# Layer 1 of a two-layer decoder: attention stages and helper threads reordered across batches, weights folded

## The chip, the cores and the metric

One core of a Trainium2 chip runs the whole decoder in one program. The metric is the device time in microseconds of that core; the median of three executions counts. All tensors are fp32 except one-hot tables, masks and an identity, which are bf16.

## The reference, cut to what matters

There are eight batches (B) of 256 tokens (T) with 256 features (D), and 16 heads of 16 features. Layer 0 (an attention, a convolved cross attention, a latent attention with a mixture of four experts) is not touched by the change. Between the layers stands a scan over the tokens of six-component line coordinates, which gives one gate per batch and token (`Gt`). Layer 1 computes, for each batch, with LN a layer norm without weights and post-norm residuals:

```
# attention ("tally" in the kernel), x = output of layer 0
q, k, v = split(x @ qkv_w.T + qkv_b)
y  = softmax(causal(q k.T / 4)) v + gate * (x @ memv_w.T + memv_b)
x2 = LN(x + y @ out_w.T + out_b)
# cross attention over 64 listed context tokens per query ("count")
cd = ctx @ W_kv_down.T ;  k, v = split(cd @ W_kv_up.T) ;  q = x2 @ W_q.T
# a key listed n times weighs n times; keys that are not listed are left out
z  = LN(x2 + (softmax over listed(q k.T / 4) v) @ W_out.T)
# feed-forward, 8 experts of width 64, two branches
Q = z @ W_Q.T ; K = cumsum(z) @ W_K.T            # the sum runs over tokens
fwd(Q, K):  sum_e w_e * ((Q V_e) * (K W_e)) U_e + w b,   w = softmax(gelu(Q r1) r2)
inv(Q @ W_inv, K @ W_inv):  the same form with its own weights
out = LN(z + ((fwd + alpha * inv) / n) @ W_O.T)   # n = number of the token
```

All products that precede an elementwise factor are linear in z or in its running sum, and all that follow are linear in the products. `W_Q V`, `W_Q W_inv V`, `W_K W`, `W_Q r1`, `U W_O` and `memv_w out_w` are therefore constant matrices.

## The kernel before, in words

Each engine (TensorE = PE, VectorE = DVE, ScalarE = ACT, GpSimd = POOL, SyncE = SP) has its own program, written out by Python generators. A stage of work is a generator per engine, and each `yield` ends a step. `weave` and `braid` take a step of a main generator and then the steps of the others that are due in proportion, the same way on each engine, so the order on every engine is fixed at build time. Semaphores link the engines.

**Attention** (`attention_pe`, `attention_dve`, `attention_act`, from L527 on) runs in slots of two heads. A slot i holds on TensorE: the scores of pair i (L573) with the mask added by an identity product (L583); the turning of the probabilities of an earlier pair into the flip bank (`flip_probs`, L620); and their product with the values into OA (`values`, L635). VectorE takes the row maxima (L752) and, in count attention, multiplies by the counts (L759). ScalarE takes the exponentials (L702, L704) and moves the flipped probabilities to SBUF (`move_probs`, L689). There are two score banks, SM[0] and SM[1], so the scores of pair i wait for the exponentials of pair i-1 (`bank_free`). Tally attention flips one slot behind the scores and has 8 + 1 + 1 = 10 slots; count attention flips two slots behind and has 11. With two flip banks ScalarE alternates exponential and move; with one bank (`early`, L709) it makes both moves and then both exponentials, and TensorE puts `values` between the two flips. Layer 1 uses two flip banks, PT[0] and PT[1]; layer 0 uses one.

**Layer 1.** `reader_*` is one chain per batch: turn X, q and k, v, the memory projection (L2428, L2430), tally attention with the hot sums between scores and flips (128 one-hot products into SC, L2451, from tables that VectorE compares, L2556, two groups of eight per slot), turn of Z and its addition (L2576), out projection, layernorm into X2, the q, k, v of the cross attention (through QF and a masking on ScalarE, L728), count attention, projection, layernorm into Zb. It has 35 steps, 21 of them attention slots. `feed_*` is the feed-forward of one batch with 22 steps: turn Zb (L359), fQ (FQ[0]), running sum and fK (FQ[1]), finv on both (FQ[2], FQ[3]), r1 on FQ[0] and FQ[2] with a gelu (L2720), eight factor products (L376, moved by L2727 and multiplied at L2759), router (L2655) and softmax, spreading the weights (L2673), the back product (L2681, L2683), scale, turn of Yb, fO added to Zb (L2702, L395), layernorm, store. It fills the banks PJ[0] and PJ[1] in turn. `stagger` runs reader 0 alone, then reader i woven with feed i-1, then feed 7 alone:

```
alone(reader(0), READER_SLOTS)
for i in range(1, B):
    weave(reader(i), READER_SLOTS, feed(i - 1), FEED_SLOTS)
alone(feed(B - 1), FEED_SLOTS)
```

**Between the layers** (L2236 to L2386) SP loads the features and, behind them in its queue, all weights of layer 1 (`arena<-lay`, 7700.5 KB). VectorE computes the scan. TensorE adds six sets of rows (L2379), the i-th when `row_ready` has come; VectorE makes rows i into the buffer of rows i-2 and waits for that set to be added (L2330).

**Helpers that the change uses from layer 0:** `Bank` (one PSUM bank shared by a thread; `claim` waits for the last release), `turn` (four transposes), `summed` (512-column residual pass and a projection on top), `scaled_out_*` (reciprocal sums spread to the heads' rows and multiplied in), `move_v_act_b`, `braid`.

## Time and profile before

| | |
|---|---|
| three timed executions | 2785.33, 2785.68, 2793.83 us; median 2785.68 |
| profiled execution | 2778.91 us; its span 2777.1 us |
| mean granted TensorE clock | 0.875 of full |
| busy: TensorE, VectorE, ScalarE, GpSimd | 82%, 50%, 35%, 13% of the span |
| layer 0 and what precedes it | 0 to about 1348 us |
| between the layers | about 1348 to 1479 us |
| layer 1 | 1479.0 to 2777.1 us |

The durations in what follows come from the profiled execution. A busy time is the time in which the engine had at least one instruction running; overlapping records of TensorE are counted once. The granted clock is a fraction of full speed, 2.4 GHz; its other level is 1.2 GHz, 0.50 in the rows. In rows of a timeline, instructions of one kind that follow each other are merged with their count. An fp32 product appears as two records, a transpose as one.

### The profile page before, as it was taken

The page shows a single profiled execution, that of the slowest core. Times are in us where ns is not written, and L with a number is a line of the kernel's source. Part 1 is how long each engine was busy: PE and PEld are TensorE (multiplying, and loading weights), DVE is VectorE, ACT ScalarE, POOL GpSimd, SP SyncE. Part 2 cuts the span into 40 slices and gives each one's busy share as a digit, 9 for nine tenths or more (in the row PEclk, how much of TensorE's full clock was granted, in tenths as well). Part 3 has the DMA queues.
Part 4 walks back from the last instruction along what each step waited for, and adds up shares of the span by engine and source line. Part 5 has one row for each costly group of instructions (what it writes and reads, how often), then busy time and mean ns, then how long its engine had stood idle before and what let it go on. Part 6 is the DMA issues. An engine that isn't in the chain of part 4 may idle for free. (4 is left out here: it accounts for less than half of the span.)

```text
span 2777.1 us, 39594 instructions
## 1 busy us (share of the span) xinstructions
PE 2281.8 (82%) x13818; PEld 1620.3 (58%) x13875; DVE 1396.8 (50%) x4005; ACT 975.9 (35%) x3080; POOL 362.1 (13%) x638
## 2 busy tenths in 40 slices
PE   8678888888898888968136788898989888898988
PEld 4356566565777655757014566665656666665755
DVE  6245546465444553221295555554656555554651
ACT  3123434444353433422002343233334333233331
POOL 1043242351414150000000000000000000000000
PEclk9667878898989988989567899999999999999997
DMA  7000000002223013446500000000000000000000
GB/s 282 8 4 1 5 8 5 8 9 77 77 82 111 24 32 113 154 158 227 155 20 10 8 2 8 6 8 5 5 8 2 8 6 9 5 8 5 1 4 4
DMA packets 50765, 116.30 MB, mean 42 GB/s; under 512 B 8192, under 2 KB 30464, under 8 KB 46976
## 3 DMA queue, kind: packets, MB, share of 16 engines
q1 hardware_dynamic: 49024, 109.49, 11.8%
q0 software_dynamic: 1536, 4.20, 0.5%
q8 instruction: 115, 1.88, 0.3%
q14 instruction: 90, 0.74, 0.1%
HBM read 90.20 MB, written 23.46 MB: 41 GB/s over the span
## 5 line engine op out<-in xcount | busy, mean ns | idle before, releaser
L689 ACT ACTIVATE PRS<-PT 128x384 f32<-128x384 f32 (+1 forms) x512 | 264.3, 521 | 476.6 <-PE PT L620 476.4
L752 DVE TENSOR_REDUCE negmax<-SM 128x2 f32<-128x512 f32 x432 | 283.8, 686 | 232.2 <-PE SM L583 168.8
L704 ACT ACTIVATE PRS<-SM,negmax 128x128 f32<-128x128 f32 x608 | 249.3, 421 | 261.5 <-DVE negmax L752 261.5
L620 PE MATMUL PT<-const_sb,PRS 128*128 128x128 f32 x1664 | 281.4, 299 | 25.6 <-ACT PRS L689 18.5
L620 PEld LDWEIGHTS PT<-const_sb,PRS 128*128 128x128 f32 x1664 | 208.2, 153 | 84.4 <-issue 55.4
L376 PE MATMUL PJ<-big,arena 128*128 128x256 f32 x832 | 216.6, 408 | 8.5 <-ACT big L2720 8.5
L2556 DVE TENSOR_SCALAR arena<-arena 128x256 bf16<-128x256 bf16 x1024 | 206.0, 282 | 0.6 <-PE SC L2451 0.6
L573 PE MATMUL SM<-KF,QM 32*128 32x256 f32 (+1 forms) x1024 | 138.1, 388 | 69.6 <-ACT PRS L702 47.6
L376 PEld LDWEIGHTS PJ<-big,arena 128*128 128x128 f32 x832 | 165.9, 205 | 44.5 <-ACT big L2720 12.0
L635 PE MATMUL OA<-PRS,VS 128*32 128x256 f32 (+1 forms) x1536 | 189.7, 372 | 0.6 <-ACT PRS L689 0.6
L573 PE MATMUL SM<-haloU,QM 32*128 32x128 f32 (+1 forms) x1056 | 172.9, 373 | 13.2 <-ACT PRS L704 10.7
L412 POOL TENSOR_TENSOR rstd_a<-var_a,const_sb 128x2 f32<-128x2 f32 x33 | 26.4, 801 | 1064.6 <-DVE var_a L425 982.7
L702 ACT ACTIVATE PRS<-SM,negmax 128x256 f32<-128x256 f32 x256 | 106.2, 479 | 137.6 <-DVE negmax L752 137.6
L573 PEld LDWEIGHTS SM<-KF,QM 32*128 32x128 f32 x1024 | 80.4, 191 | 115.4 <-ACT PRS L702 64.7
L573 PEld LDWEIGHTS SM<-haloU,QM 32*128 32x128 f32 x1056 | 129.4, 212 | 28.5 <-ACT PRS L704 15.1
L573 PE MATMUL SC<-haloU,QM 32*128 32x128 f32 (+1 forms) x480 | 113.5, 392 | 35.5 <-ACT PRS L704 35.5
L2451 PE MATMUL SC<-arena,identb 128*128 128x256 bf16 x1024 | 125.7, 274 | 0.2 <-DVE arena L2556 0.2
L635 PEld LDWEIGHTS OA<-PRS,VS 128*32 128x32 f32 x1536 | 76.6, 115 | 83.6 <-issue 48.2
L704 ACT ACTIVATION_READ_ACCUMULATOR PRS<-SM,negmax 128x1 f32 x608 | 124.9, 205 | 0.0
L583 PE MATMUL SM<-masks,identb 128*128 128x256 bf16 (+1 forms) x377 | 107.1, 338 | 10.1 <-issue 10.1
L2451 PEld LDWEIGHTS SC<-arena,identb 128*128 128x128 bf16 x1024 | 100.1, 98 | 16.3 <-DVE arena L2556 0.5
L1829 PE MATMUL PJ<-arena 128*128 128x128 f32 x800 | 104.9, 290 | 5.6 <-ACT gate_s L1845 4.6
(521 smaller groups left out, 3972.8 us busy)
## 6 DMA issues: line engine op xcount, KB each, us to landing
arena<-lay SPq DMA_DIRECT2D x50, 1024.0 KB, 4.9
arena<-lay SPq DMA_DIRECT2D x1, 7700.5 KB, 32.6
rows<-OT SPq DMA_DIRECT2D x2, 3456.0 KB, 32.3
arena<-lay SPq DMA_DIRECT2D x1, 3862.0 KB, 19.6
arena<-rows SPq DMA_DIRECT2D x25, 128.0 KB, 2.5
arena<-lay SPq DMA_DIRECT2D x25, 128.0 KB, 5.0
rows<-arena SPq DMA_DIRECT2D x25, 128.0 KB, 4.4
rows<-OT SPq DMA_DIRECT2D x1, 2432.0 KB, 21.9
```

Of the source, the lines that this page charges most:

```text
L376: ins = pe.matmul(bank[:, m * T:(m + 1) * T], w[:, k, m0 + m * P:m0 + (m + 1) * P], actT[:, k, :], start=k == 0, stop=k == KT - 1)
L573: pe.matmul(banks[s % NB][:, o:o + cols], query(h, t, a), keys, start=t == 0 and a == taps[0], stop=False, skip_group_check=True)
L583: pe.matmul(bank[:, lo:hi], identb[:], flat(mask)[:, lo:hi], start=False, stop=True, skip_group_check=True).then_inc(S("scores_ready"), 1)
L620: ins = pe.transpose(bank[:, o:o + P], PR[n % 4][:, t, k * P:(k + 1) * P], ident)
L635: ins = pe.matmul(OA[strip(h), g * T + lo:(g + 1) * T], hs.values[:, k, h, :], src, start=h % 2 == 0 and k == 0, stop=h % 2 == 1 and k == ...
L689: act.activation(dst, src, ACT.Copy).then_inc(S("probs_moved"), 1)
L702: ins = act.activation(dst, src, ACT.Exp, bias=negmax[:, h, r:r + 1])
L704: ins = act.activation(dst, src, ACT.Exp, bias=negmax[:, h, r:r + 1], accum_out=rsum[:, t, h:h + 1])
L752: st.post(dve.tensor_reduce(negmax[:, ORDER[s], :], two(banks[s % NB]), AX.X, ALU.max, negate=True), S("max_ready"))
L1829: ins = pe.matmul(bank[:, m * P:(m + 1) * P], WU[i][:, k, f:f + P], XST[i][:, k, :], start=k == 0, stop=k == KT - 1)
L2451: ins = pe.matmul(SC[:, t * T:(t + 1) * T], identb[:], oneh[g % 2][:, j, :], start=j0 + j == 0, stop=j0 + j == NI - 1)
L2556: ins = dve.tensor_scalar(oneh[g % 2][:, j, :], iotab, idx[:, t, j0 + j:j0 + j + 1], None, ALU.is_equal)
```

## The change

1. Layer 1 has a new order (`layer1_schedule`). The main line holds attention only: tally attention of batch i, then count attention of batch i-1, in turn. The rest is cut into threads per batch that are braided beside it: `start` (5 steps: turn X, q, k, v, memory), `hot` (19 steps, one group of eight each), `middle` (4: from tally attention to X2 and its turn), `ask` (4: the q, k, v of the cross attention), `end` (3: from count attention to Zb), `feed` (2 + 8 + 8).
2. Tally and count attention have their own queries, keys, values and outputs, and one flip bank, PT[0]. The threads have a bank each: "a" PT[1] (start, end, r1), "j" PJ[0] (middle, ask), "f" PJ[1] (feed).
3. Between the layers, 31 units (`folds`) on TensorE and ScalarE multiply weights once: fV and fW by fQ, fK and finv; r1 by fQ, and by finv and fQ into the place of fQ; fU and b8 by fO and alpha; memv and its bias by out_w. 16 units stand ahead of the first set of rows, three ahead of each of the others. The products fQ, fK, finv (twice), fO, one of the r1 inputs, and the turns of Yb and Z have no place in the loop any more. The weights' load now waits for the features (`feat_in`).
4. SP loads X two batches ahead into two buffers; queries are masked by ScalarE straight from PSUM.

```diff
-            yield from attention_pe(pe, "tally", 2 * i, 2 * i, counted, KF[:, :, 1:T + 1], add_hot)
+        TALLY = Heads(QM, VS, YT[:], rinv, S("asked_t"), [PT[0]])
+        COUNT = Heads(QM_count, VS_count, ZT[:], rinv_c, S("asked_k"), [PT[0]])
+        OPEN, JOIN, TURN, END = 5, 4, 4, 3
+        GROUPS_HOT = TT * NI // 8
+        HOT_FIRST, HOT_REST, FEED_FIRST, FEED_PART = 10, GROUPS_HOT + 3 - 10, 2, 8
...
+            def ended(i):
+                return (("end", i, END), ("feed", i, FEED_FIRST)) if i >= 0 else ()
...
+            chains(opened(0))
+            tally(0, (("hot", 0, HOT_FIRST + HOT_REST),))
+            chains((("middle", 0, JOIN),), opened(1))
+            for i in range(1, B):
+                tally(i, (("ask", i - 1, TURN),), fed(i - 3), ended(i - 2), (("hot", i, HOT_FIRST),))
+                count(i - 1, (("middle", i, JOIN),), opened(i + 1), fed(i - 2), (("hot", i, HOT_REST),))
+            chains((("ask", B - 1, TURN),), fed(B - 3), ended(B - 2))
+            count(B - 1, fed(B - 2))
+            chains(fed(B - 2), ended(B - 1))
+            chains((("feed", B - 1, 2 * FEED_PART),))
...
         def feed_pe(pe, i, ba, bf):
+            for bank_of, name in ((ba, "r1"), (bf, "fQ")):
+                bank_of.fill(columns(pe, bank_of.claim(pe), k3(w1(name), 2), XF), "act")
...
-                ru.fill(columns(pe, bank, k3(w1(f"fW{br}"), 2), FQ[2 * br + 1], 2 * j * P))
+                bf.fill(columns(pe, bf.claim(pe), k3(w1(f"fW{br}"), 2), XC, 2 * j * P), "act")
                 yield
-                rd.fill(columns(pe, bank, k3(w1(f"fV{br}"), 2), FQ[2 * br], 2 * j * P))
+                bf.fill(columns(pe, bf.claim(pe), k3(w1(f"fV{br}"), 2), XF, 2 * j * P), "dve")
...
         def start_dve(dve, st, i, ba):
+                ins = dve.scalar_tensor_tensor(Xi[:, t, :], bank[:, t * D:(t + 1) * D], Gt[:, t, i:i + 1], Xi[:, t, :],
+                                               ALU.mult, ALU.add)
...
+            def fold_pe(pe, first, last):
+                for u in range(first, last):
+                    needs, _, (pe_part, _) = folds[u]
+                    if u == 0:
+                        pe.wait_ge(S("lay1_in"), 16)
+                    if max(needs, u - 1) > 0:
+                        pe.wait_ge(S("folded"), max(needs, u - 1))
+                    pe_part(pe, FOLD[u % 2]).then_inc(S("fold_full"), 1)
+
+            def fold_act(act):
+                for u, (_, both, (_, act_part)) in enumerate(folds):
+                    act.wait_ge(S("fold_full"), u + 1 + both)
+                    act_part(act, FOLD[u % 2]).then_inc(S("folded"), 1)
...
                 for i in range(6):
+                    fold_pe(pe, 0 if i == 0 else 16 + 3 * (i - 1), 16 + 3 * i)
                     pe.wait_ge(S("row_ready"), i + 1)
```

The whole of each unit is a turn (four transposes and a move) or a product of two 128-row halves (two passes of 512 columns, or four of 256, and a move), alternating between PT[0] and PT[1].

## Rows read from the trace of the kernel before

**Rows 1.** Page, busy time and share of the span, count of instructions, by engine.

```profile
PE 2281.8 (82%) x13818; PEld 1620.3 (58%) x13875; DVE 1396.8 (50%) x4005; ACT 975.9 (35%) x3080; POOL 362.1 (13%) x638
```

**Rows 2.** Windows: length, busy (count) PE PEld DVE ACT POOL, clock, DMA, GB/s.

```profile
1479.00:1499.70 20.70, 14.54 (x46) 9.60 (x46) 2.15 (x7) 4.64 (x11) 0.00 (x0) 0.73 0.10 33
1499.70:1542.80 43.10, 37.97 (x320) 27.02 (x322) 37.73 (x148) 20.75 (x81) 0.00 (x0) 0.92 0.01 1
...
1562.00:1603.50 41.50, 31.60 (x206) 18.48 (x208) 21.70 (x81) 20.63 (x49) 0.00 (x0) 0.88 0.01 3
...
1927.10:2082.00 154.90, 136.35 (x834) 97.70 (x839) 87.41 (x297) 56.64 (x158) 2.07 (x3) 0.96 0.02 6
...
1941.00:1996.00 55.00, 51.69 (x388) 38.39 (x388) 40.33 (x153) 26.61 (x89) 0.00 (x0) 1.00 0.01 1
...
2016.00:2068.60 52.60, 46.10 (x291) 30.51 (x294) 28.80 (x94) 22.85 (x54) 0.00 (x0) 1.00 0.03 6
...
2703.20:2777.10 73.90, 59.41 (x206) 43.77 (x206) 15.82 (x34) 8.07 (x13) 0.69 (x1) 0.78 0.01 4
```

**Rows 3.** TensorE's waits in 1927.1 to 2082.0: us in total, times, longest.

```profile
PE PJ L359 <- DVE Zb L428: 8.9, 2, 4.4
PE SM L573 <- ACT PRS L702: 5.8, 5, 2.2
PE SM L359 <- DVE X L428: 2.3, 1, 2.3
```

**Rows 4.** TensorE's groups of instructions in 1927.1 to 2082.0, by shape.

```profile
L376 PE MATMUL PJ<-big,arena 128*128 128x256 f32 x104 | 26.4, 399 | 0.9 <-ACT big L2720 0.9
...
L395 PE MATMUL PJ<-arena,ZT 128*128 128x256 f32 x8 | 1.9, 379 | 0.0
...
L2702 PE MATMUL PJ<-Zb,const_sb 128*128 128x512 f32 x2 | 1.1, 644 | 0.0
...
L359 PE MATMUL PJ<-const_sb,Yb 128*128 128x128 f32 x4 | 0.7, 287 | 0.7 <-DVE Yb L2801 0.7
```

**Rows 5.** Timeline, a slot of batch 0's count attention: start, length, merged instructions.

```profile
1576.75 1.13 PE L573 MATMUL SM<-KF,QM 32*128 32x256 f32 x8 [1.35 <-ACT PRS L702]
...
1578.25 1.04 PE L620 MATMUL PT<-const_sb,PRS 128*128 128x128 f32 x8
1578.97 0.84 ACT L702 ACTIVATE PRS<-SM,negmax 128x256 f32<-128x256 f32 x2 [1.78 <-DVE negmax L752]
...
1579.22 1.06 PE L635 MATMUL OA<-PRS,VS 128*32 128x256 f32 x8
...
1579.69 0.60 ACT L689 ACTIVATE PRS<-PT 128x512 f32<-128x512 f32 x1
...
1581.08 1.13 PE L573 MATMUL SM<-KF,QM 32*128 32x256 f32 x8 [0.80 <-ACT PRS L702]
```

**Rows 6.** Windows of two rounds of layer 0, columns as in rows 2.

```profile
530.33:642.81 112.48, 97.42 (x678) 68.40 (x680) 63.67 (x151) 51.42 (x182) 38.80 (x71) 0.86 0.03 8
...
769.97:911.34 141.37, 130.12 (x925) 100.97 (x928) 64.01 (x163) 64.03 (x239) 37.99 (x71) 0.93 0.28 92
```

**Rows 7.** Window, instructions on PJ alone: PE, PEld, DVE, ACT, clock, DMA, GB/s.

```profile
1927.10:2082.00 154.90, 49.77 (x207) 36.44 (x207) 12.51 (x21) 5.26 (x10) 0.96 0.02 6
```

**Rows 8.** Timeline, the last feed-forward, where its factor products begin.

```profile
2719.81 7.14 PE L376 MATMUL PJ<-big,arena 128*128 128x256 f32 x32 [1.02 <-ACT big L2720]
```

**Rows 9.** Page, DMA issues: tile, queue, count, KB each, us to landing.

```profile
arena<-lay SPq DMA_DIRECT2D x1, 7700.5 KB, 32.6
```

**Rows 10.** Timeline between the layers.

```profile
1375.96 0.96 DVE L2271 TENSOR_TENSOR arena<-big 128x768 f32<-128x768 f32 x1 [29.51 <-DMA Z<-gate_d]
...
1418.10 3.78 PE L2379 MATMUL SM<-arena,const_sb 128*128 128x512 f32 x4 [72.28 <-DVE arena L2330]
...
1431.55 1.76 DVE L2330 TENSOR_TENSOR arena<-arena,big 128x1536 f32<-128x1536 f32 x1
```

More of the change, by code:

```diff
@@ new lines, in start_dve @@
+        def start_dve(dve, st, i, ba):
+            yield from idle(4)
+            bank = ba.take(dve, "dve")
+            Xi = X1s[i % 2]
+            for t in range(TT):
+                ins = dve.scalar_tensor_tensor(Xi[:, t, :], bank[:, t * D:(t + 1) * D], Gt[:, t, i:i + 1], Xi[:, t, :],
+                                               ALU.mult, ALU.add)
+                ba.release(st, ins, "dve") if t else st.post(ins)
+            st.settle()
+            st.post(dve.tensor_tensor(Xi[:], Xi[:], w1("out_b").unsqueeze(1).broadcast_to([P, TT, D]), ALU.add), S("biased"))
+            yield
@@ L2677, in back @@
-            def back(ring, br):
-                bank = ring.claim(pe)
-                for t in range(TT):
+            for br in range(2):
+                for j in range(2):
+                    bank = bf.claim(pe)
+                    for m in range(2):
+                        ins = pe.matmul(bank[:, m * T:(m + 1) * T], k3(w1("sel8"), 4)[0:KE, 2 * j + m, :], WT8[:, br, :],
+                                        start=True, stop=True)
+                    bf.fill(ins, "dve")
+                    yield
@@ L2740, in feed_dve @@
             Yf = Yb[i % 2]
-            move(dve, st, rd, XF)
+            bank = bf.take(dve, "dve")
+            bf.release(st, dve.tensor_copy(XF, two(bank)), "dve")
             st.settle()
@@ L2859, in _, with thread @@
+                def thread(what, i):
+                    return {"start": lambda: start_pe(pe, i, ba), "middle": lambda: middle_pe(pe, i, bj),
+                            "ask": lambda: ask_pe(pe, i, bj), "end": lambda: end_pe(pe, i, ba),
+                            "hot": lambda: hot_pe(pe, i), "feed": lambda: feed_pe(pe, i, ba, bf)}[what]()
+                layer1_schedule(attend, thread)
             @block.vector
             def _(dve):
-                sta, stb = Steps(dve, S("dve")), Steps(dve, S("dve_b"))
@@ new lines, in _, with attend, thread @@
+                for k in range(KT):
+                    st.post(dve.tensor_tensor(qkb_masked[:, 2 * k:2 * k + 2], parq[:],
+                                              w1("qkb")[:, k:k + 1].broadcast_to([P, 2]), ALU.mult), S("qkb_ready"))
+                st.settle()
+                def attend(kind, i, inst):
+                    return attention_dve(dve, st, kind, inst, i, TALLY if kind == "tally" else COUNT, Cn[i % 2])
+                def thread(what, i):
+                    return {"start": lambda: start_dve(dve, sta, i, ba), "middle": lambda: middle_dve(dve, stj, i, bj),
+                            "ask": lambda: ask_dve(dve, stj, i, bj), "end": lambda: end_dve(dve, sta, i, ba),
+                            "hot": lambda: hot_dve(dve, sth, i), "feed": lambda: feed_dve(dve, stf, i, bf)}[what]()
@@ L2877, with thread @@
+                def thread(what, i):
+                    return {"start": lambda: start_act(act, sa, i, ba), "middle": lambda: idle(JOIN),
+                            "ask": lambda: ask_act(act, sj, i, bj), "end": lambda: idle(END),
+                            "hot": lambda: idle(HOT_FIRST + HOT_REST), "feed": lambda: feed_act(act, sf, i, ba, bf)}[what]()
+                layer1_schedule(attend, thread)
 def kernel(**inputs):
```

679 lines of the change are left out of this document (382 added, 297 removed).

## The prediction, made before the result was known

> **What bounds the kernel now.** I read the page's busy shares first: TensorE is busy 82% of the span, VectorE 50% [rows 1]. The windows then place the stages. Layer 1 runs from 1479.0 us to the end at 2777.1, so 1298.1 us: batch 0 alone (1479.0 to 1612.3), seven woven rounds, and the last feed-forward alone (73.9 us). A round, from 1927.1 to 2082.0, has TensorE busy for 136.4 of 154.9 us at a granted clock of 0.96, VectorE for 87.4 and ScalarE for 56.6 [rows 2]. TensorE is the bound and 18.5 us of a round are its gaps. The waits name most of them: the layernorm of Zb, which stands at a seam with nothing else to issue, the layernorm of X, and the exponentials that have to free a score bank before the next pair's scores [rows 3]. So two things can be gained in a round: TensorE work, and gaps.
>
> **TensorE work that goes.** Every 256-column fp32 product shows as two records. The 104 records from big are 26.4 us, 0.254 us each [rows 4]. Of these the change drops the projections by fK and by finv (twice) and one of the two r1 columns; from XF it issues two (r1, fQ) where it issued one. Net: 4 calls of 8 records, 32 x 0.254 = 8.1 us. With fO folded into fU, its 8 records go (1.9), and so do the 512-column pass of Zb (1.1) and the turn of Yb (0.7) [rows 4]. The turn of Z goes in the same way, another 0.7: memv is folded with outw and VectorE adds it to X. Sum 12.5 us a batch, 100 us over eight. Its bounds: it is all of the gain if TensorE stays the bound, and near nothing where another chain sets the slot (next part).
>
> **VectorE and ScalarE.** About ten passes of 512 columns (moves of FQ, Y, YF, Yb, QF, sums of Z) go from VectorE's 87.4 us and two come back; ScalarE gains a handful of one-column copies that release banks. Both stay well under TensorE. VectorE's sixteen compare groups are now spread one to a slot over tally and count instead of two to a tally slot, which evens its queue. I cost these at nothing; the cover is TensorE's 124 us per round, and if VectorE's queue showed (three layernorms a batch issued in line, each ahead of the next row maximum) it would be some 2 us each, 6 us a round.
>
> **The seams.** Before, 14 of the reader's 35 slots are seams (what a round of 154.9 us has beside the woven tally, 55.0, and count, 52.6 [rows 2]: 47.3 us) where the reader is a chain of fill, move, fill. In the new order only tally and count attention stand in the main line, and open, middle, ask, end are threads beside the other batch's attention. The two layernorm waits (8.9 shown for two that touch this window, so 4.5 a round, and 2.3 [rows 3]) get an attention slot between fill and use. They go; what is late next is the exponential wait.
>
> **One flip bank in place of two.** This is the price. In a count slot with nothing beside it, scores to scores takes 4.33 us (1576.75 to 1581.08 [rows 5]), with ScalarE alternating exponential, move, exponential, move. With one bank, ScalarE's order is move, move, exponential, exponential, and the second flip waits for the first move. From the same rows: scores and mask 1.50 (to the first flip at 1578.25), flip 0.52 (half of 1.04), values 1.06 (they cover the 0.60 of the first move), flip 0.52, move 0.1 + 0.60, two exponential pairs 1.68, semaphores 0.1: 6.1 us. Queued behind the wait on TensorE are the threads' matmuls, and behind those the next scores. A tally slot by the same sum, with three transposes and moves of 0.5, is 5.6. So attention alone cannot be shorter than 6 x 6.1 + 2 x 4.1 + 3 x 2.0 = 50.8 us (count, 11 slots) and about 47 us (tally, 10 slots), against 41.5 and 43.1 now when alone [rows 2]. Full rounds carry more TensorE work than this floor: 124 us against 98. In a loaded slot about 3.0 to 3.6 us is attention's own and the other 3.3 us, on average, is threads; the chain leaves 2.5 us open, so only the lean slots (I find one in tally, two in count with under 1.5 us beside) show it. Bounds: 0 if all is hidden, 1.75 us x 16 slots = 28 us a round if none is. I take 5 to 6 us.
>
> **The round.** Layer 0 of this kernel already runs with one flip bank and threads beside. Its round from 530.33 to 642.81 has 97.4 us of TensorE at clock 0.86, which is 83.8 us of full clock, in 112.5 us; the one from 769.97 to 911.34 has 130.1 at 0.93, 121.0, in 141.4 [rows 6]. A line through the two gives 0.78 us of time per us of work. Layer 1's new round has (136.4 - 12.5) x 0.96 = 118.9, so 140 us, against 154.9 now. The bottom-up sum (124 of work, 6 of flip chain, 6 of layernorms, 2 of slot edges) says 138. I take 140.
>
> **The whole layer.** Open 19; tally 0 alone with its hot sums 47 (floor above); middle 0 with open 1, 16 (open alone is 20.7 now [rows 2], and the new one is five short steps of both). Round 1 has no feed and no end. The feed is all that writes PJ, 49.8 us a round [rows 7]; without what goes (12.5 less the 0.7 of Z) it is 38. For end's sum I estimate 5 of work. So 77.7 of full clock and 108 us by the line. Round 2 lacks the second half of a feed (17): 126. Rounds 3 to 6: 4 x 140 = 560. Round 7 has no open (14.5 at clock 0.73 [rows 2], so 11 to 12): 131. Then ask 7 with half a feed and end 6, a chain of eight steps: 33; count 7 with half a feed 54; half a feed and end 7: 31. The last feed alone starts at its factors: today 2719.81 to 2777.1, 57 us [rows 8]; one bank in place of two costs about 0.9 us (a 0.60 move and its semaphores) on eight factor fills, +7, and behind the back product the turn, two moves, the Zb pass and fO go, about -10: 54, and 3 for the store. Sum 1182 against 1298: -116.
>
> **The stage between the layers.** 31 folds are added on TensorE and ScalarE, both nearly idle there while VectorE computes. The lay1 transfer, 32.6 us from issue to landing [rows 9], now starts only when feat has landed (1375.96 at the latest, VectorE's first product), but alone on the queues, and lands near 1397 by my estimate; TensorE is otherwise free until 1418.10 [rows 10]. Sixteen folds come before the first row sum: 4 turns at 0.6 and 12 products of two 512-column passes. At full clock a pass is half the 1.6 us that the six records from 1418.10 show at half clock (3.78 us for four of them), so 27 us in all with the start at the low clock: done near 1425, row sum to 1428. VectorE first needs it at its third row, 1431.55 [rows 10]. Later groups of three folds (5.5 us) fit beside each 7.6 us row. I take 0; bounds -2 (feat lands alone) and +17 (all folds at half clock: 45 us, VectorE waits once).
>
> **Sum.** The profiled execution took 2778.9 us (span 2777.1 and 1.8 around it): 2778.9 - 116 = 2663. The median of the three timed runs, 2785.7, lies 6.8 above it, so I forecast 2670.
>
> **Rivals.**
> (a) The gaps close entirely. For: the woven tally stretch 1941.0 to 1996.0 is busy 51.7 of 55.0 at clock 1.00 [rows 2]. Then a round is 118.9 / 0.94 = 127; 13 us less, over the equivalent of 5.5 full rounds 72, so 2598. Against: two flip banks there.
> (b) The clock. Layer 0's lighter round was granted 0.86 while layer 1's is granted 0.96 [rows 2, 6], with the one-bank form in the former. If the new rounds get 0.86, work is 118.9 / 0.86 = 138 and with layer 0's 11.3 us of gaps 149.5: +9.5 x 5.5 = +52, 2722. Against: the heavier layer 0 round had 0.93. The Trainium skill, "TensorE: Matmul & The Clock Gate", section "A second HAM failure mode: psum-queue depth-cycling", says that cycling through PSUM banks leaves small idles between groups, so that the clock swings between its two levels; by that rule this rival would win, and the trace bears it out for the light round only.
> (c) Slower than before: the flip chain is not covered. Each thread's matmuls are issued behind flip b, hence after the time in which they could help, and add to the slot. Then a round is 98 + 71 (124 less the 53 that are attention's own) = 169: +29 x 5.5 = +160, 2830. It decides from a round of 161 us on. For: TensorE is strictly in order. Against: now, threads issued in the same place lengthen count from 41.5 to 52.6 us while adding 14.5 us of TensorE work [rows 2].
> (d) The folds run late: +17, 2687. Or a waiting fold holds up the row sums further; the cost stays in that stage.
>
> **How the numbers follow.** Forecast 62% (its own range 2635 to 2700), (a) 13%, (b) 13%, (d) 7%, (c) 5%. 2605 to 2735 leaves out (c), and about half of (a) and a little of (b). A change of 0.3%, 8 us, is about what can be told from none. Only (c) and the tail of (b) come near the old time: faster 0.93, same 0.03, slower 0.04.
>
> **What would show it.** A round (from the last layernorm of one Zb to the next) of 136 to 145 us with TensorE busy about 124; L376 records from big and ZT gone or fewer by 32 and 8; no wait of PJ on Zb or of SM on X over 1 us; PT flips waiting on ScalarE's move for under 1 us each, ScalarE moves in pairs; score waits on exponentials growing in lean slots. Between the layers, the first row sum before 1430. Wrong if: a round above 150, a clock under 0.9 in the rounds, or a VectorE gap at the third row.

## The result, and the profile after

The changed kernel takes 2642.02 us, median of four runs (2633.05 to 2646.53), against 2785.51 for the kernel before (2756.17 to 2793.83, four runs beside it): a ratio of 0.950, with a 95% interval of 0.942 to 0.957. The forecast was 2670 in a range of 2605 to 2735. The profiled execution took 2646.27 us, with a span of 2644.5. Some executions of a kernel show a lower granted clock and take longer; medians and ranges below are of all executions, ratios leave those out. Line numbers after L360 are one higher than before, those of the reader's helpers more.

Busy time by engine, from the page of the changed kernel, answers to [rows 1]:

```profile
PE 2243.5 (85%) x13569; PEld 1574.3 (60%) x13637; DVE 1341.9 (51%) x3927; ACT 998.1 (38%) x3145; POOL 363.0 (14%) x639
```

TensorE lost 38 us of busy time while the span lost 133: 79.5 us less in layer 1 (1125.8 to 1046.2), 33.6 more between the layers (27.9 to 61.4, the folds) and 7.7 more before them, in the same 7113 records. Windows of the changed kernel, columns as in [rows 2]: open 0, tally 0, the first seam, a whole round, its tally part, its count part, the seam before the last count, the last feed:

```profile
1479.00:1499.70 20.70, 13.30 (x32) 8.18 (x32) 1.19 (x3) 3.57 (x8) 0.95 (x1) 0.58 0.14 42
1499.70:1554.70 55.00, 48.92 (x339) 31.33 (x338) 39.13 (x154) 22.07 (x83) 0.00 (x0) 0.82 0.01 3
1554.70:1571.00 16.30, 13.61 (x56) 9.11 (x54) 3.89 (x11) 4.27 (x11) 0.70 (x1) 1.00 0.04 16
1932.63:2065.54 132.91, 125.17 (x783) 87.86 (x792) 80.08 (x286) 57.31 (x162) 2.07 (x3) 0.97 0.02 8
1932.63:1995.92 63.29, 58.87 (x378) 41.07 (x380) 38.03 (x123) 27.44 (x94) 1.38 (x2) 0.97 0.03 10
1995.92:2065.54 69.62, 66.30 (x408) 46.78 (x413) 42.05 (x165) 29.86 (x68) 0.69 (x1) 0.98 0.01 5
2455.00:2490.00 35.00, 29.70 (x97) 20.69 (x98) 10.71 (x23) 4.27 (x9) 0.69 (x1) 0.76 0.00 0
2590.00:2644.50 54.50, 36.44 (x135) 25.50 (x133) 10.06 (x24) 4.72 (x10) 0.69 (x1) 0.85 0.01 5
```

A round fell from 154.9 us [rows 2] to 132.9, by 22.0. Half of that, 11.2 us, is busy time of TensorE (136.4 to 125.2); the other half is its gaps (18.5 to 7.7 us). Busy time multiplied by the granted clock is a rough measure of the work in full-clock us, and I use it below: 130.9 before, 121.4 now.

TensorE's waits of that round (us in total, times, longest) answer to [rows 3]:

```profile
PE SM L574 <- ACT PRS L705: 2.6, 2, 1.8
PE PT L621 <- ACT PRS L690: 1.8, 3, 0.8
PE SM L574 <- ACT PRS L703: 1.3, 1, 1.3
PE SM L584 <- issue: 1.1, 7, 0.2
PE PJ L1209 <- DVE arena L2915: 0.9, 1, 0.9
```

The waits of 8.9 and 2.3 us for the layernorms of Zb and X are gone (the 0.9 us before a turn of Zb is a wait for the thread's bank, not for a layernorm). What is late next is what the prediction named: the exponentials before the next scores (3.9 us in all), and, new, flips that wait for ScalarE's move of the flip before them (1.8 us). The waits for exponentials fell too. In the round before they were 8.0 us, 5.8 on the line of [rows 3] and 2.2 on this one:

```profile
PE SM L573 <- ACT PRS L704: 2.2, 4, 1.1
```

The groups of column products by shape in the changed kernel's round (busy us, mean ns) answer to [rows 4]:

```profile
L377 PE MATMUL PJ<-OT,arena 128*128 128x256 f32 x40 | 9.5, 378 | 0.0
...
L377 PE MATMUL PJ<-big,arena 128*128 128x256 f32 x32 | 8.2, 401 | 0.0
...
L377 PE MATMUL PT<-OT,arena 128*128 128x256 f32 x8 | 1.9, 379 | 0.0
```

Between the layers, the timeline of the changed kernel (start, length) shows the first row sum at 1425.04, straight behind the sixteenth fold, and VectorE without a pause:

```profile
1423.22 1.98 PE L2413 MATMUL PT<-PRS,X 128*128 128x512 f32 x4 [0.69 <-ACT arena L2417]
1425.04 1.88 PE L2526 MATMUL SM<-arena,const_sb 128*128 128x512 f32 x4
...
1425.37 1.76 DVE L2332 TENSOR_TENSOR arena<-arena,big 128x1536 f32<-128x1536 f32 x1
```

### The profile page after: what moved, and what is told of

Same layout as the page of the kernel before. It is cut to its first block and busy times, and to the rows that moved or that the text cites. A ratio compares the mean times of both kernels' runs of the same rounds, so it can differ in the third digit from the quotient of the medians.

```text
span 2644.5 us, 38948 instructions
## 1 busy us (share of the span) xinstructions
PE 2243.5 (85%) x13569; PEld 1574.3 (60%) x13637; DVE 1341.9 (51%) x3927; ACT 998.1 (38%) x3145; POOL 363.0 (14%) x639
## 5 line engine op out<-in xcount | busy, mean ns | idle before, releaser
L621 PE MATMUL PT<-const_sb,PRS 128*128 128x128 f32 x1664 | 314.2, 307 | 40.0 <-ACT PRS L690 33.9
L574 PE MATMUL SM<-haloU,QM 32*128 32x128 f32 (+1 forms) x1056 | 182.2, 388 | 12.0 <-ACT PRS L705 9.5
L574 PEld LDWEIGHTS SM<-haloU,QM 32*128 32x128 f32 x1056 | 136.5, 223 | 27.3 <-ACT PRS L705 13.0
L2774 PE MATMUL SC<-arena,identb 128*128 128x256 bf16 x1024 | 139.1, 279 | 2.7 <-DVE arena L2756 2.7
L636 PE MATMUL OA<-PRS,big 128*32 128x256 f32 (+1 forms) x1024 | 136.5, 393 | 3.0 <-ACT PRS L690 3.0
L636 PE MATMUL OA<-PRS,VS 128*32 128x256 f32 (+1 forms) x1024 | 127.6, 378 | 0.6 <-ACT PRS L690 0.6
L574 PEld LDWEIGHTS SC<-haloU,QM 32*128 32x128 f32 x480 | 87.3, 231 | 44.9 <-ACT PRS L705 39.9
L1830 PE MATMUL PJ<-arena 128*128 128x128 f32 x800 | 107.0, 294 | 5.6 <-ACT gate_s L1846 4.6
L413 POOL TENSOR_TENSOR rstd_a<-var_a,const_sb 128x2 f32<-128x2 f32 x25 | 20.9, 837 | 659.8 <-DVE var_a L426 577.1
L1830 PEld LDWEIGHTS PJ<-arena 128*128 128x128 f32 x800 | 103.4, 210 | 8.8 <-issue 7.2
L1837 PE MATMUL PJ<-arena 128*128 128x256 f32 x400 | 90.5, 381 | 9.2 <-ACT gate_s L1859 9.2
L413 POOL TENSOR_TENSOR rstd_e<-var_e,const_sb 128x2 f32<-128x2 f32 x16 | 11.2, 697 | 600.9 <-DVE var_e L426 445.0
```

The source lines that it names most:

```text
L574: pe.matmul(banks[s % NB][:, o:o + cols], query(h, t, a), keys, start=t == 0 and a == taps[0], stop=False, skip_group_check=True)
L621: ins = pe.transpose(bank[:, o:o + P], PR[n % 4][:, t, k * P:(k + 1) * P], ident)
L636: ins = pe.matmul(OA[strip(h), g * T + lo:(g + 1) * T], hs.values[:, k, h, :], src, start=h % 2 == 0 and k == 0, stop=h % 2 == 1 and k == ...
L1830: ins = pe.matmul(bank[:, m * P:(m + 1) * P], WU[i][:, k, f:f + P], XST[i][:, k, :], start=k == 0, stop=k == KT - 1)
L2774: ins = pe.matmul(SC[:, t * T:(t + 1) * T], identb[:], oneh[g % 2][:, j, :], start=j0 + j == 0, stop=j0 + j == NI - 1)
```

## The experiments

Twelve runs in three groups, each beside the kernel before. "Old order" is the kernel before with one thing changed; all others are the changed kernel with one thing changed. The first four rows are the first group, the next four the second, the last four the third. The changed kernel stands only in the third group and in the result above, so its distance from runs of the first two groups compares medians of different groups; the kernel before had 2774.9, 2780.4 and 2777.0 us in the three.

| run | median (range) us | ratio to before, 95% interval |
|---|---|---|
| e_old_folded | 2762.95 (2754.84 to 2792.17) | 0.997 [0.993, 1.000] |
| e_old_oneflip | 3054.07 (3037.93 to 3064.58) | 1.095 [1.087, 1.103] |
| e_seams | 2719.92 (2702.35 to 2720.66) | 0.976 [0.970, 0.983] |
| e_tail | 2660.93 (2644.81 to 2669.03) | 0.954 [0.947, 0.961] |
| e_work_back | 2694.52 (2692.71 to 2711.62) | 0.972 [0.967, 0.977] |
| e_two_flips | 2713.31 (2687.47 to 2730.86) | 0.973 [0.967, 0.979] |
| e_hot_tally | 2814.64 (2773.59 to 2827.82) | 1.016 [1.012, 1.021] |
| e_no_folds | 2641.22 (2633.49 to 2656.07) | 0.951 [0.946, 0.956] |
| e_changed_again | 2637.80 (2627.95 to 2662.00) | 0.955 [0.947, 0.962] |
| e_shift | 2642.95 (2625.36 to 2654.41) | 0.955 [0.948, 0.961] |
| e_last_banks | 2627.30 (2624.33 to 2642.38) | 0.951 [0.945, 0.957] |
| e_both | 2620.79 (2616.26 to 2631.63) | 0.948 [0.942, 0.954] |

### The folds alone, in the old order

The kernel before with the folds between the layers, and the feed of folded weights in its old reader:

```diff
+                    fold_pe(pe, 0 if i == 0 else 16 + 3 * (i - 1), 16 + 3 * i)
...
-                ins = dve.tensor_scalar(Z[:, t, :], bank[:, t * D:(t + 1) * D], Gt[:, t, i:i + 1], None, ALU.mult)
+                ins = dve.scalar_tensor_tensor(Xin[:, t, :], bank[:, t * D:(t + 1) * D], Gt[:, t, i:i + 1], Xin[:, t, :],
+                                               ALU.mult, ALU.add)
```

> The kernel before with the folded weights alone: old order, old banks, two flip banks; the feed has 16 steps instead of 22. Theory 'work and gaps add up': TensorE work falls by the same 11 to 12.5 us a round as in the changed kernel, the seams keep their gaps (18.5 us a round), so a round goes from 155.6 to about 144 and the last feed alone from 74 to about 57: some 97 us less, 2688. Rival 'the fold does it all': a round near 133 and about 2640. Rival 'the fold only widens the gaps of the old order': a round above 150 and 2735 or more.

My theory fell, and the third of the expectations holds by its times (a round above 150, the whole above 2735). The removed work is gone from the trace, but not the time. Windows of a round, of two stretches of 5 us in its count part, and of the last feed:

```profile
1923.83:2079.39 155.56, 134.55 (x788) 93.98 (x788) 82.57 (x287) 55.44 (x156) 2.07 (x3) 0.90 0.02 6
2018.00:2023.00 5.00, 2.83 (x14) 1.29 (x10) 2.67 (x10) 1.57 (x4) 0.00 (x0) 0.72 0.00 0
2023.00:2028.00 5.00, 3.65 (x16) 2.63 (x16) 2.67 (x10) 2.54 (x6) 0.00 (x0) 0.50 0.00 0
...
2700.60:2757.60 57.00, 43.42 (x160) 32.88 (x160) 13.11 (x29) 5.59 (x10) 0.69 (x1) 0.77 0.01 5
```

The round has 788 records where [rows 2] has 834, and a busy time times clock of 121.1 us, as much as the changed kernel's 121.4. But it is as long as before, and not mainly through wider gaps, which are 21.0 us against 18.5. Its busy time is only 1.8 us shorter (134.55 against 136.35), because the clock is 0.90 in place of 0.96. One place to see it is the count slots that now have no product of the feed beside them: TensorE is busy 2.83 and 3.65 of 5 us there and is granted 0.72 and 0.50, so that the rest runs slower. The other rounds of this trace agree (155.0 to 155.6 us, 154.8 to 157.5 before), and so does the mean clock of its ten executions, 0.848 to 0.863 against 0.860 to 0.882. The only gain to be seen is at the end, where the last feed takes 57.0 us instead of 73.9.

### One flip bank, in the old order

```diff
-            counted = Heads(QM, VS, YT[:], rinv, S("q_ready"), PT)
+            counted = Heads(QM, VS, YT[:], rinv, S("q_ready"), [PT[1]])
```

> The kernel before with one flip bank (PT[1]) instead of two, nothing else. Theory: the second flip waits for the first move, and both moves stand ahead of the exponentials, partly covered by the hot sums and the feed's matmuls: a round 8 to 12 us longer, 8 batches, +80 us (2865). Rival 'all hidden': within 10 us of before. Rival 'nothing hidden', 1.75 us on 16 slots: +28 us a round, about 3000.

The price was more than three times what I put (279 us by the medians, where I expected 80), and above the rival's bound of 3000 us for nothing hidden. Windows of a round and of its count part:

```profile
2024.40:2218.30 193.90, 162.42 (x838) 109.11 (x838) 88.14 (x296) 57.61 (x158) 2.07 (x3) 0.84 0.02 5
...
2135.00:2206.00 71.00, 60.98 (x280) 35.45 (x278) 27.10 (x90) 22.05 (x50) 0.00 (x0) 0.76 0.00 1
```

And the timeline of one count slot in it, scores to scores 8.60 us (2158.76 to 2167.36):

```profile
2158.76 1.74 PE L573 MATMUL SM<-KF,QM 32*128 32x256 f32 x8 [2.14 <-ACT PRS L702]
2160.43 1.03 PE L583 MATMUL SM<-masks,identb 128*128 128x512 bf16 x2
...
2161.26 1.06 PE L620 MATMUL PT<-const_sb,PRS 128*128 128x128 f32 x4
2162.25 1.92 PE L635 MATMUL OA<-PRS,VS 128*32 128x256 f32 x8
...
2164.10 1.12 PE L620 MATMUL PT<-const_sb,PRS 128*128 128x128 f32 x4
2165.14 2.50 PE L2673 MATMUL PJ<-arena 8*128 8x256 f32 x5
...
2167.36 0.80 PE L573 MATMUL SM<-KF,QM 32*128 32x256 f32 x2
```

Four transposes take 1.06 us where eight took 1.04 in [rows 5]: this slot runs at the lower level of 1.2 GHz. The order flip, values, flip, two moves and only then the exponentials leaves little beside it; the lean slot is granted the lower clock, and that makes the chain itself longer. The second flip does not wait for the first move in this slot: it stands behind `values` (1.92 us), which covers the move, and the next scores wait for the exponentials behind the second move. My 6.1 us had been summed at the upper level. Of the 39 us that the round is longer (193.9 against 154.9), 26 are busy time of the same products at a clock of 0.84 in place of 0.96, and 13 are gaps, most of them waits for exponentials (17.9 us against 8.0). Other rounds of this trace took 187 to 196 us. So the price of one flip bank is no constant: in the new order all waits that it could cause are the 5.7 us shown above.

### The seams put back

```diff
-                count(i - 1, (("middle", i, JOIN),), opened(i + 1), fed(i - 2), (("hot", i, HOT_REST),))
+                chains((("middle", i, JOIN),), opened(i + 1))
+                count(i - 1, fed(i - 2), (("hot", i, HOT_REST),))
```

> The changed kernel, but in each round the threads middle and open stand alone between tally and count attention, beside each other, instead of being braided into count attention. Theory: a chain of five steps takes 16 us (it took 16.3 behind tally attention of batch 0), count attention loses 13.6 us of matmuls but cannot fall under its own floor of about 52, so a round is 3 to 6 us longer: +20 to +45 us against the changed kernel. Rival 'the weave is what closed the gaps': +11 us a round, +75. Rival 'it was only the flip chain's spare time that was filled': 0.

Windows of its seam, its count part, its tally part and the round of these three:

```profile
1877.90:1893.98 16.08, 13.47 (x62) 9.40 (x61) 5.25 (x18) 5.34 (x12) 0.69 (x1) 1.00 0.05 16
1893.98:1951.40 57.42, 54.60 (x357) 37.07 (x355) 37.65 (x150) 25.07 (x58) 0.00 (x0) 0.97 0.01 1
1951.40:2018.90 67.50, 63.24 (x375) 43.51 (x374) 37.42 (x120) 26.80 (x94) 1.38 (x2) 0.90 0.03 10
1877.90:2018.90 141.00, 131.32 (x789) 89.98 (x789) 80.32 (x288) 57.21 (x162) 2.06 (x3) 0.94 0.02 7
```

Seam and count part together take 73.5 us where the changed kernel's count part takes 69.6: 3.9 more, within the 3 to 6 of my theory. What it lacked is 4.2 us in the tally part, whose order is unchanged (67.5 us at a clock of 0.90, 63.3 at 0.97 in the changed kernel). There is little idle time in it: 2.6 us in the seam, and 9.7 in the round against 7.7. Of the 8.1 us that the round is longer, 6.1 are busy time of the same products (131.3 against 125.2), at a clock of 0.94 in place of 0.97. Rounds of this trace differ (137.9 to 147.1 us); over the six from count 0 to count 6 the mean is 9.0 us longer than in the changed kernel. The kernel is slower by about 80 by the medians (2719.9 against 2637.8 to 2642.0), which is the rival's +75; the profiled execution was this kernel's fastest, and its span is 56 longer.

### The drain in another order

```diff
-            chains((("ask", B - 1, TURN),), fed(B - 3), ended(B - 2))
-            count(B - 1, fed(B - 2))
-            chains(fed(B - 2), ended(B - 1))
+            chains((("ask", B - 1, TURN),), (("end", B - 2, END),))
+            count(B - 1, fed(B - 3), (("feed", B - 2, FEED_FIRST),))
+            chains((("feed", B - 2, FEED_PART),), (("end", B - 1, END),))
+            chains((("feed", B - 2, FEED_PART),), (("feed", B - 1, FEED_FIRST),))
```

> The changed kernel with another order behind the last round: only ask 7 and end 6 stand alone; the second half of feed 5 and the first two steps of feed 6 go beside count attention of batch 7; feed 6's two halves run beside end 7 and the first steps of feed 7. The same instructions. Theory: TensorE is busy 115 of the 135 us from 2455 to 2590 at a clock of 0.76 to 0.94, and count 7 there has a slot floor under which 5 to 10 us more work hides: 5 to 14 us less. Rival 'feed 6 alone is a chain of fills and moves': no change or longer.

Nothing was gained: the theory fell and the rival holds. Some 20 us are lost by the medians, though the ranges overlap; in the traces, from the end of count 6 to the end of the program, it takes 206 us where the changed kernel takes 187 and 183 in two executions. From the end of the last count, the first window of this kernel and the second of the changed one:

```profile
2541.00:2667.10 126.10, 94.44 (x318) 66.42 (x316) 25.60 (x62) 11.71 (x25) 2.07 (x3) 0.77 0.02 7
```

```profile
2549.90:2644.50 94.60, 69.62 (x244) 48.60 (x244) 22.14 (x52) 8.23 (x16) 2.07 (x3) 0.82 0.02 6
```

The last count is 9 us earlier, but 25 us more of busy TensorE stand behind it, in chains, at a clock of 0.77. Work moved out of an attention's cover into a drain is paid at the drain's rate.

### Two thirds of the work put back

```diff
-                bf.fill(columns(pe, bf.claim(pe), k3(w1(f"fW{br}"), 2), XC, 2 * j * P), "act")
+                columns(pe, bf.claim(pe), k3(w1(f"fW{br}"), 2), XC, 2 * j * P)
+                bf.fill(columns(pe, bf.bank, k3(w1(f"fW{br}"), 2), XC, 2 * j * P), "act")
```

> The changed kernel with each of the four feature-weight factor products of a batch's feed issued twice into its bank (the first is overwritten), so that 32 matmuls of L377, about 8.1 us of TensorE by the mean of 0.254 us of that row, come back into every round, with no other step moved. My theory (in the woven order the threads cover the attention's chain and the clock stays near its upper level, so that work counts one for one): rounds go from 132.9 to 139 to 142 us, the last feed grows by 3 to 8, and the whole by 55 to 75 us, to about 2705. Rival (the round is set by the chain of scores, flips and values, and the work fits into the 7.7 us of gaps): rounds stay at 133 to 135 and the whole under 2660. Second rival (more work keeps the clock higher than 0.97, or fewer waits): in between, +30 to +50 us.

Windows of the count part and of a whole round:

```profile
2002.68:2077.12 74.44, 72.08 (x441) 51.51 (x441) 41.77 (x163) 29.66 (x68) 0.69 (x1) 1.00 0.02 4
1937.37:2077.12 139.75, 133.14 (x822) 93.83 (x821) 80.07 (x286) 57.25 (x163) 2.07 (x3) 0.98 0.02 7
```

8.0 us more of busy TensorE (133.14 against 125.17) are 6.8 us more of time (139.75 against 132.91), and the waits for exponentials, moves and layernorm are the changed round's, to the tenth. The whole kernel is 52 to 57 us slower than the changed one by the medians (2642.0 and 2637.8), in place of the 65 of eight full charges. The theory holds for the round (139 to 142 us expected), at 0.80 to 0.87 of time per us of work; the whole lies at the lower edge of its range. The gap-bound rival is out.

### Two flip banks, in the new order

```diff
-        TALLY = Heads(QM, VS, YT[:], rinv, S("asked_t"), [PT[0]])
-        COUNT = Heads(QM_count, VS_count, ZT[:], rinv_c, S("asked_k"), [PT[0]])
+        TALLY = Heads(QM, VS, YT[:], rinv, S("asked_t"), PT)
+        COUNT = Heads(QM_count, VS_count, ZT[:], rinv_c, S("asked_k"), PT)
...
-                ba, bj, bf = (Bank(*spots[name]) for name in ("a", "j", "f"))
+                bj, bf = (Bank(*spots[name]) for name in ("j", "f"))
+                ba = bj
```

> The changed kernel with both attentions' flips over two banks, as in the kernel before; the bank that the ask and feed threads (named a) had is taken from them, and they share one with the join (named j). If one flip bank costs what my prediction took (5 to 6 us a round, seven rounds), the rounds fall from 132.9 to about 127 to 129 in their attention and some of it comes back as waits of the threads for their shared bank: 2600 to 2650 in all. Rival (the threads cover the flips' chain already, so the second bank buys nothing, and the threads lose the overlap of their own fills): rounds of 134 to 140, 2650 to 2700 in all, and a larger idle row of TensorE before the threads' fills. The last feed and the stage between the layers should not differ by more than 3 us either way, except that the two threads meet on one bank there as well.

Slower than the changed kernel by some 70 us, more than either theory had. The profiled execution lies at the top of this kernel's range, so I read only its waits in a round of 138.8 us:

```profile
PE SM L574 <- ACT PRS L705: 3.7, 2, 2.5
PE PJ L377 <- DVE YT L1460: 1.7, 1, 1.7
PE PJ L1209 <- DVE rT L1456: 1.4, 1, 1.4
...
PE PT L621 <- ACT PRS L690: 0.2, 1, 0.2
```

The wait of flips for moves went from 1.8 to 0.2 us, the waits for exponentials hardly moved (3.7 us against 3.9), and the threads that share a bank wait more. The edit does two things at once, so the second bank's own worth isn't isolated, and what makes this kernel 70 us slower is not shown.

### All hot sums beside the tally

```diff
-                tally(i, (("ask", i - 1, TURN),), fed(i - 3), ended(i - 2), (("hot", i, HOT_FIRST),))
-                count(i - 1, (("middle", i, JOIN),), opened(i + 1), fed(i - 2), (("hot", i, HOT_REST),))
+                tally(i, (("ask", i - 1, TURN),), fed(i - 3), ended(i - 2), (("hot", i, HOT_FIRST + HOT_REST),))
+                count(i - 1, (("middle", i, JOIN),), opened(i + 1), fed(i - 2))
```

> The changed kernel with all 19 steps of the hot sums beside the tally attention; the count attention then has none of them. My theory (the tally part is the shorter one in the round, 63.3 against 69.6 us, and TensorE is busy 93 to 95% in both, so only the sum of the work counts): the tally part grows by what the count part loses and the round stays within 2 us of 132.9, 2635 to 2665 in all, unless the compares of VectorE fall behind in tally 0, which then grows from 55.0 to 58 to 65 at its low clock. Rival (the balance between the parts counts, as each part ends with its slowest thread): rounds of 128 to 130, 2615 to 2625 in all. Rival on the other side (two compares a slot gate the scores that stand behind them in every tally): rounds of 138 or more, 2685 or more.

The rival on the other side, and far beyond its bound. By its ratio it is slower than the kernel before, though by less than 2% and with ranges that overlap; the profiled execution, 2773.6 us, was its fastest. Windows of a round, its tally part and its count part:

```profile
1964.81:2121.82 157.01, 135.99 (x791) 91.80 (x789) 81.08 (x286) 57.09 (x163) 2.06 (x3) 0.91 0.02 6
1964.81:2059.11 94.30, 77.75 (x446) 52.54 (x444) 50.86 (x182) 26.80 (x94) 1.38 (x2) 0.86 0.02 7
2059.11:2121.82 62.71, 58.24 (x347) 39.26 (x345) 30.22 (x105) 30.29 (x69) 0.69 (x1) 1.00 0.02 5
```

The waits in its tally part, first TensorE's and then VectorE's:

```profile
PE SC L2774 <- DVE arena L2756: 15.0, 8, 4.1
```

```profile
DVE negmax L753 <- PE SM L584: 12.0, 7, 3.8
```

Nine more groups of sums lengthen the tally part by 31 us and shorten the count part by 7. Neither engine is full. TensorE's next scores stand behind hot sums that wait for VectorE's second compare, and VectorE's next compares stand behind a row maximum that waits for those scores: two programs, each waiting for the other, at a clock that falls to 0.86. Two groups in a slot are not enough for this by themselves. The kernel before has two in every tally slot, and its woven tally (1941.0 to 1996.0) has no wait of the sums for a compare; tally 0 of the changed kernel has two with hardly anything beside them and waits 2.2 us. What these rounds add is the other threads' work on both engines in the same slots; no run tests that alone.

### Without the folds

```diff
-                fold_act(act)
...
-                    fold_pe(pe, 0 if i == 0 else 16 + 3 * (i - 1), 16 + 3 * i)
```

> The changed kernel without its 31 folds between the layers, neither TensorE's products nor ScalarE's moves of them: the products of weights that the layer then reads are left out of the computation, and every instruction of the layer keeps its shape. If the folds are hidden behind the rotation's products and VectorE's row chain, as the two traces say by their ends (1477.45 before, 1477.33 after), the time stays within 4 us of the changed kernel's: 2638 to 2650. Rival (they lie on the path and only something else came back that hid it; 31 products of about 0.25 us with their moves, 15 to 28 us by their window): 2615 to 2630. A third way: without them the clock at the layer's start is lower and the first tally longer, 2645 to 2655.

This kernel leaves out the products of weights that layer 1 then reads, so it computes other values in the same instructions. 2641.2 us against 2642.0 and 2637.8 of the changed kernel: the folds are hidden. The stage says the same. From VectorE's first product between the layers to the layer's first turn of X it takes 106.5 us without the folds, and 105.5 and 107.0 in two executions of the changed kernel.

### The hot sums half a round later, and the last feed over two banks

The changed kernel ran once more in this group. In the shifted version (and in the one with both edits) the count mask is read before the last groups of its tallies are in, so that they leave out a part of the counts.

> The changed kernel itself, once more, so that the versions run beside it are compared on the same chip: 2633 to 2650, rounds of 132.9.

```diff
-            tally(0, (("hot", 0, HOT_FIRST + HOT_REST),))
+            tally(0, (("hot", 0, HOT_FIRST),))
...
-                tally(i, (("ask", i - 1, TURN),), fed(i - 3), ended(i - 2), (("hot", i, HOT_FIRST),))
-                count(i - 1, (("middle", i, JOIN),), opened(i + 1), fed(i - 2), (("hot", i, HOT_REST),))
+                tally(i, (("ask", i - 1, TURN),), fed(i - 3), ended(i - 2), (("hot", i - 1, HOT_REST),))
+                count(i - 1, (("middle", i, JOIN),), opened(i + 1), fed(i - 2), (("hot", i, HOT_FIRST),))
```

> The changed kernel with each batch's 19 steps of the hot sums moved half a round later in the order: ten beside the count attention of the batch before and nine beside the tally of the batch after (ten beside tally 0, nine in the seam before the last count, where TensorE was busy 29.7 of 35.0 us at a clock of 0.76). My theory after the run with all 19 steps beside the tally (39 of 50 us busy there, a product waiting 1.94 us for the second compare of its slot): tally 0 too has two steps in a slot, so its 55.0 us fall to 47 to 50 with one, the middle rounds stay within 1 us, the last seam grows by 0 to 4: 3 to 8 us off the changed kernel. Rival (tally 0 is slow only for the low clock at the layer's start, 0.82): it falls by less than 2 us, and the last seam's nine steps add 3 to 8: 2 to 6 us more than the changed kernel.

From the first turn of the layer to count 0, the changed kernel (this group's run) and then the shifted one:

```profile
1471.20:1613.80 142.60, 121.66 (x702) 78.04 (x704) 71.85 (x264) 53.37 (x189) 0.70 (x1) 0.79 0.03 9
```

```profile
1477.70:1618.70 141.00, 115.08 (x638) 72.95 (x640) 56.62 (x188) 52.87 (x188) 0.70 (x1) 0.78 0.02 8
```

64 records fewer and 1.6 us gained: my reading of two compares in a slot fell, and the rival stands as far as the start goes. With less to do beside tally 0 TensorE waits instead (gaps of 25.9 us against 20.9), at the same low clock (0.78 and 0.79), and the whole is 5 us above the changed kernel by the medians, within the ranges. A cause for that clock is not shown.

```diff
+            bw = ba if i == B - 1 else bf
...
-                bf.fill(columns(pe, bf.claim(pe), k3(w1(f"fW{br}"), 2), XC, 2 * j * P), "act")
+                bw.fill(columns(pe, bw.claim(pe), k3(w1(f"fW{br}"), 2), XC, 2 * j * P), "act")
```

> The changed kernel with the last batch's feed alone alternating between its own bank and the bank a, which is free by then. In the trace of the changed kernel a fill of the last feed follows the one before by its own 2.0 us and 0.85 to 1.0 us of wait for the copy that frees the bank; 13 such waits can be covered, some 9 to 12 us of the 54.5: 2630 to 2635 in all. Rival (the clock there, 0.85, falls or rises with the filling, so the records get longer): 2 to 5 us won. Rival on the other side: the products of VectorE and the copies of ScalarE become the chain and nothing is won, within 2 us.

Timeline of TensorE in the last feed of the changed kernel (this group's run), and then with two banks:

```profile
2583.27 1.97 PE L377 MATMUL PJ<-big,arena 128*128 128x256 f32 x8 [1.02 <-ACT big L2843]
2586.24 2.00 PE L377 MATMUL PJ<-OT,arena 128*128 128x256 f32 x8 [1.00 <-ACT gate_s L2851]
```

```profile
2579.58 1.89 PE L377 MATMUL PT<-big,arena 128*128 128x256 f32 x8
2581.31 1.89 PE L377 MATMUL PJ<-OT,arena 128*128 128x256 f32 x8
```

The distance of two fills falls from 2.97 to 1.73 us. From the end of the last count's scores to the end of the program, the same two kernels in that order:

```profile
2532.10:2639.10 107.00, 80.71 (x319) 55.69 (x318) 27.81 (x75) 14.01 (x28) 2.07 (x3) 0.84 0.02 5
```

```profile
2531.40:2623.20 91.80, 75.31 (x317) 55.24 (x317) 27.80 (x75) 14.02 (x28) 2.07 (x3) 0.85 0.02 6
```

15.2 us less in the trace, 10.5 by the medians (2627.3 against 2637.8; the ranges overlap). By the medians that is in the 9 to 12 us expected. It computes all that the reference asks and has the lowest median of such versions, 0.951 [0.945, 0.957] of the kernel before in its group, where the changed kernel has 0.955 [0.947, 0.962].

> Both of the two moves (the hot sums half a round later, the last feed over two banks) on the changed kernel: if they add up, 12 to 20 us less than it, some 2622 to 2632; if the hot sums' shift gains nothing, that of the last feed alone.

2620.8, 17.0 below the changed kernel beside it, as if the two edits added up; but its tail is that of the last version (91.9 us), and the 6.5 us between their medians lie inside both ranges (2616 to 2632 and 2624 to 2642), so what the shift adds can't be told.

## Why the prediction was right, and where its steps were off

**The mechanism** was right: TensorE is the bound, its removed work and its closed gaps are the gain, and of the rivals only (a) came part of the way. One sign was named too high (a round of 136 to 145 us, where 132.9 came), and one did not come (waits for exponentials growing: they fell from 8.0 to 3.9 us). The 28 us between forecast and median are 17 on the profiled execution (2663 against 2646.3) and 11 of scatter: I added 6.8 because the profiled run of before was a fast one, and that of after lies 4.2 above its median.

**TensorE's work**, predicted 12.5 us a round of busy time: 11.2 came. Its largest term, 32 records of column products for 8.1 us, is to be seen: before, 104 from big and 8 from XF (26.4 and 1.9 us), now 32 + 40 + 8 (8.2, 9.5, 1.9), so 32 fewer and 8.7 us. What I had not seen is that this term has no fixed value. In the old order the same folds changed the round by nothing (154.9 to 155.6) because the freed time became a lower clock and, for 2.5 us, gaps; in the new order two thirds of it, put back, cost 6.8 us a round. In the rounds the folds pay only together with the new order. The new order with two thirds of the work back still gains 86 us (2780.4 to 2694.5 in its group). If the last third, 4.4 us a batch, costs at the same 0.85, some 30 us, the new order alone brings about 56 of the 144 (an estimate, not run).

**The seams**: their waits went as predicted. By the run with a woven seam back, weaving it away is worth 8 to 9 us a round, three quarters of it as shorter busy time of the same products at a higher clock and not as gaps, which my sum had no term for.

**One flip bank**, put at 5 to 6 us a round: the waits on exponentials and moves now sum to 5.7 us, but 8.0 us of waits on exponentials stood there before, so only the 1.8 us for moves are surely new. Part of the rest has another source: ScalarE itself waited 5.9 us in this round for row maxima of VectorE. The term's price in the new order is not isolated by any run, and that 5.7 is near my number shows nothing. Its reasoning failed: the slot sum of 6.1 us held the clock fixed, and a slot that does show the chain was 8.6 us long.

**The round**, 140 us by the line through layer 0: the step that was too high, by 7 us. The line carried layer 0's clock (0.86 and 0.93) and its gaps (11 to 15 us) into a round that was granted 0.97 and has 7.7 us of gaps. Work of 121.4 us over 132.9 is a share of 0.91; rival (a) had put 0.94. The sum from below, 138, put 14 us of gaps on 124 of work. Its three terms (flip chain 6, layernorms 6, slot edges 2) are 6 us too much together. The rows don't part them, but no wait on a layernorm is among the 7.7 us. Thus (a) was half right: rounds 3 to 6 took 534.6 us against 560. The rival on the clock (b) did not come in this kernel's rounds, at 0.97; runs above show a lower clock in rounds of other orders, 0.84 to 0.94. By the Trainium skill, "TensorE: Matmul & The Clock Gate", section "A second HAM failure mode: psum-queue depth-cycling", small idles between groups of products, in a kernel that cycles through PSUM banks, made the clock swing between its levels. The old order with one flip bank agrees with it: gaps of 31.5 in 193.9 us, a clock of 0.84. The new order has the same one bank, gaps of 7.7 in 132.9 us and a clock of 0.97. Between these two the low clock goes with the gaps, and the number of banks is the same.

**The whole layer** came out at 1165.5 us against 1182. The ends were too low and the middle too high: open and tally 0 took 75.1 against 66 (clock 0.58 and 0.82; the floor of 47 was a full-clock figure), rounds 1 and 2 took 105 and 121 (108 and 126), round 7 123.8 (131), ask 7 with count 7 94.9 (87), and the seam behind it 40 (31), again at clocks of 0.76 to 0.79; the last feed took 54.5 (57). I sized all chains at full clock, and these did not get it. Part of the closeness of the whole is luck: the rounds were put some 41 us too long and the rest some 24 too short.

**The stage between the layers**, put at 0: the first row sum was predicted for 1428 and came at 1425.04, and the run without folds has the same time. Rival (d) is out, and so is (c) in this kernel. The old order with one flip bank did lose as much (+39 us a round, (c) had put 29), but two thirds of it at a lower clock, which (c) did not have.

## What to carry to other kernels

Removed work pays only where its engine is the bound in that very stretch: before counting it, ask what else sets the length of the slot it leaves, and expect that the clock may fall there. Put independent threads beside every dependent chain, one step to a slot; in the run with all hot sums beside the tally, a second step of the same kind in each slot left two engines waiting for each other. Size starts, seams and drains at the clock that their own windows show, and give the last, lone chain all the banks that its finished neighbours leave.

## What the runs showed that I had not expected

Three times the granted clock went against an edit. 12 us of work taken from an old-order round left its length as it was, with the clock at 0.90 in place of 0.96. One bank less cost 39 us a round where the moves and semaphores that it exposes, 0.7 us in each of 16 slots by [rows 5], are some 11 (an estimate). Nine groups of sums moved by half a round cost 24 us a round. In each, TensorE's busy time times its clock stayed near that of the faster kernel (121.1, 136.4 and 123.8 against 121.4, 130.9 and 121.4), so the loss is not added work but the same work at a lower clock, together with gaps: 26 and 13 us of the 39 for the flip bank, 11 and 13 of the 24 for the sums. Why the clock falls as far as it does in each is not shown.
